# Row maxima of attention handed over in halves, and the expert weights of layer 0 loaded and turned at another place

## What is computed

```python
# layer 0 attention (layer 1: the same with a causal mask, without the three normalizations)
q, k, v = layernorm(x @ Wq + bq), layernorm(x @ Wk + bk), layernorm(x @ Wv + bv)   # per head
scores = einsum('bhqd,bhkd->bhqk', q, k) * HD ** -0.5
x = x + einsum('bhqk,bhkd->bqhd', softmax(scores), v).reshape(b, s, 256) @ Wo + bo
# layer 0 cross attention: top 32 of 77 scores, softmax over them, weighted values, output projection
# layer 0 experts
probs = softmax(einsum('bsd,ed->bse', x, router_w) + router_b)
y = take_along_axis(einsum('bsd,eod->bseo', x, expert_w) + expert_b, argmax(probs), axis=2)
x = x + y * max(probs)
```

## Time and profile before

| What | us |
|---|---|
| median of three runs (lowest, highest) | 1895.42 (1893.15, 1896.32) |
| the profiled execution | 1903.1 |
| its span | 1901.4 |
| attention of layer 0, first fill to last output half | 118.3 to 563.6 |
| from there to the first top-k instruction | 563.6 to 590.1 |
| attention of layer 1, first fill on | from 1132.1 |

### The profile page before, as it was taken

How to read it: one execution, slowest core, us unless ns; L and a number is a source line. 1 busy time by engine, 2 the same in 40 slices (tenths; PEclk the granted TensorE clock), 3 DMA queues, 4 the chain that set the end, 5 groups by cost and what they waited for, 6 DMA issues and landing times. The chain is left out here.

```text
span 1901.4 us, 27565 instructions
## 1 busy us (share of the span) xinstructions
PE 1543.4 (81%) x8891; PEld 836.8 (44%) x8892; DVE 1226.4 (64%) x4679; ACT 941.4 (50%) x1856; POOL 515.6 (27%) x419
## 2 busy tenths in 40 slices
PE   5858999999973688888877767999987883369997
PEld 3511222222222566666666533333326672136664
DVE  6978887877505999999992446777725567501211
ACT  2823777777663555555544432666673652111211
POOL 1791000000001466555553150111211332240111
PEclk9956999999897899999987876999998996679999
DMA  6293334221010000000000186355402122531110
GB/s 210 82 210 58 45 47 99 41 41 18 26 32 13 1 2 1 1 1 1 1 2 1 34 232 89 46 69 111 90 3 88 15 40 36 202 106 36 45 45 8
DMA packets 112679, 106.01 MB, mean 56 GB/s; under 512 B 45523, under 2 KB 86555, under 8 KB 112542
## 3 DMA queue, kind: packets, MB, share of 16 engines
q1 hardware_dynamic: 107281, 93.83, 23.4%
q0 software_dynamic: 2640, 6.31, 0.9%
q10 hardware_dynamic: 2624, 4.19, 0.7%
HBM read 68.56 MB, written 36.41 MB: 55 GB/s over the span
## 5 line engine op out<-in xcount | busy, mean ns | idle before, releaser
L1113 DVE TENSOR_REDUCE arena<-banks 128x2 f32<-128x1024 f32 (+1 forms) x448 | 481.2, 1107 | 162.2 <-PE banks L954 105.6
L1045 ACT ACTIVATE arena<-banks 128x512 f32<-128x512 f32 (+3 forms) x896 | 440.1, 557 | 188.1 <-PE banks L993 181.5
L954 PE MATMUL banks<-arena 96*128 96x512 bf16 (+3 forms) x896 | 286.4, 397 | 55.3 <-DMA arena<-v 26.8
L993 PE MATMUL banks<-arena 98*128 98x512 bf16 (+3 forms) x896 | 272.4, 364 | 9.3 <-ACT arena L1045 6.8
L1005 PE MATMUL banks<-arena 128*32 128x512 f32 (+3 forms) x1792 | 220.8, 565 | 12.6 <-ACT arena L1045 6.5
L1712 DVE MATCH_REPLACE8 arena<-arena 128x77 f32<-128x77 f32 x1024 | 213.8, 223 | 0.0
L954 PEld LDWEIGHTS banks<-arena 96*128 96x128 bf16 x896 | 80.8, 102 | 238.3 <-DVE arena L1113 137.7
L993 PEld LDWEIGHTS banks<-arena 98*128 98x128 bf16 x896 | 82.5, 98 | 188.5 <-ACT arena L1045 124.4
L1602 POOL TENSOR_SCALAR arena<-arena 128x256 f32<-128x256 f32 x32 | 39.2, 1224 | 449.8 <-DVE arena L1689 449.8
L2498 DVE COPY arena<-banks 128x1024 f32<-128x1024 f32 x23 | 28.2, 1225 | 198.6 <-PE banks L2432 198.6
L1704 DVE MAX8 arena<-arena 128x8 f32<-128x77 f32 x1024 | 149.5, 224 | 0.9
(11 more groups left out here) (279 smaller groups left out, 2465.3 us busy)
## 6 DMA issues: line engine op xcount, KB each, us to landing
arena<-parts SPq DMA_DIRECT2D x192, 128.0 KB, 7.4
parts<-arena SPq DMA_DIRECT2D x24, 512.0 KB, 5.3
arena<-in_L_ffn_W SPq DMA_DIRECT2D x12, 1024.0 KB, 10.9
v<-arena SPq DMA_DIRECT2D x32, 256.0 KB, 2.3
arena<-v SPq DMA_DIRECT2D x16, 512.0 KB, 11.1
arena<-in_L_ffn_W ACTq DMA_DIRECT2D x4, 1024.0 KB, 9.4
arena<-sorted_rows SPq DMA_DIRECT2D x23, 129.0 KB, 2.2
arena<-sorted SPq DMA_DIRECT2D x23, 128.0 KB, 2.1
```

Of the source, the lines that this page charges most:

```text
L954: mm = pe.matmul(bank[:, 0:w], qst[r][0:KS, j, i * P:(i + 1) * P], kst[r][0:KS, j, kb * BANK:kb * BANK + w], start=True, stop=not diag)
L993: pe.matmul(bank, kst[r][0:KM, j, kt * P:(kt + 1) * P], qst[r][0:KM, j, half * BANK + lo:(half + 1) * BANK], start=True, stop=True).then_i ...
L1045: act.activation(prob[:, gi % 2 * G + j, lo:BANK], PS[:, 4 + n % 3, 0:BANK - lo], ACT.Exp, scale=SCALE).then_inc(sem(s + "_exp"), 1)
L1113: dve.tensor_reduce(m2[u % 2][:, 2 * pair:2 * pair + 2, i, kb], PS[:, 2 * (n % 2):2 * (n % 2) + 2, 0:w], AX.X, ALU.max).then_inc(sem(s + " ...
```

## The change

Row maxima are handed over in two halves of four query tiles each. There are two MAX entries in a unit in place of one, each with its three small VectorE steps on half the elements, its own turn and copy, and four row DMAs (one for each head, 4 KB) in place of one. TensorE waits for the first half's rows before the unit's first group and for the second half's before the first group of the second query half. This holds for both layers. SyncE loads only unit 1 at the start, and unit 2 after both row halves of unit 0. In later units the load of unit u + 2 comes after the second half's rows of unit u.

In layer 0 alone the ring is dealt out anew: the second pass of unit 0 starts after fill 24 of unit 0 (`first_due`), and unit u ends at fill 28 of unit u + 1. In units 0 and 7 a quarter of the unit takes the entries up to MAX of the second half, and the rest is spread over the remainder.

The expert weights of layer 0 have memory of their own (`RAW_AT`), are loaded within attention at u = 4, and all eight are turned in iteration 0 (TURNS). Only the bias is loaded after attention.

```diff
@@ -856,7 +858,7 @@
             mx = [R.f32(G * TB).rearrange("p (j t) -> p j t", j=G) for _ in range(2)]
-            mh = [R.bf16(2 * G * TB) for _ in range(2)]
+            mh = [R.bf16(G * TB) for _ in range(2)]
             mT = [R.bf16(P) for _ in range(2)]
@@ -867,8 +869,11 @@
-            def hilo(u):
-                return mh[u % 2].rearrange("p (c j t) -> p c j t", c=2, j=G)
+            HT = TB // 2
+            HALF_FILLS = sum(1 for f in unit_fills if f[0] < HT)
+
+            def hilo(half):
+                return mh[half].rearrange("p (j c t) -> p c j t", c=2, j=G)
@@ -877,11 +882,24 @@
             for u in range(NU):
-                feed.insert(feed.index((FILL, u, NF - 1)) + (5 if u < NU - 1 else 1), (MAX, u, 0))
+                feed.insert(feed.index((FILL, u, HALF_FILLS - 1)) + 5, (MAX, u, 0))
+                feed.insert(feed.index((FILL, u, NF - 1)) + (5 if u < NU - 1 else 1), (MAX, u, 1))
+            first_due = feed.index((FILL, 1, AHEAD) if causal else (FILL, 0, 24))
             due = []
             for u in range(NU):
-                due.append(feed.index((FILL, u + 2, AHEAD)) if u + 2 < NU else len(feed))
-            first_due = feed.index((FILL, 1, AHEAD))
+                n, f = (u + 2, AHEAD) if causal else (u + 1, NF - 4)
+                due.append(feed.index((FILL, n, f)) if n < NU else len(feed))
+            early = 0.25
+
+            def goal(u, past):
+
+                at0 = due[u - 1] if u else first_due
+                if u in (0, NU - 1) and not causal:
+                    soon = max(at0, feed.index((MAX, u, 1)) + 1)
+                    if past <= early:
+                        return at0 + round((soon - at0) * past / early)
+                    return soon + round((due[u] - soon) * (past - early) / (1 - early))
+                return at0 + round((due[u] - at0) * past)
@@ -896,9 +914,9 @@
                         past += width(gi) / G
-                        goal = at0 + round((due[u] - at0) * past / WORK)
-                        ring += feed[at:goal]
-                        at = goal
+                        upon = goal(u, past / WORK)
+                        ring += feed[at:upon]
+                        at = upon
                         if j == 2 and gi in (1, last_of[0] + 2):
@@ -913,18 +931,26 @@
                 sp.wait_ge(sem(q + "_parts"), PARTS_ST)
-                for u in range(1, NST):
-                    load_unit(sp, l, u)
+                load_unit(sp, l, 1)
                 sp.wait_ge(sem(s + "_ones"), NST)
...
-                    sp.wait_ge(sem(s + "_red"), entry[MAX, u, 0] + 1)
-                    sp.dma_start(qst[u % NST][KS:KM], mT[u % 2][0:2 * G * TB]).then_inc(sem(s + "_rows"), 16)
-                    if 1 <= u <= NU - NST:
+                    for half in range(2):
+                        sp.wait_ge(sem(s + "_red"), entry[MAX, u, half] + 1)
+                        for j in range(G):
+                            sp.dma_start(qst[u % NST][KS:KM, j, half * BANK:(half + 1) * BANK], mT[half][j * 2 * HT:(j + 1) * 2 * HT]
+                                         ).then_inc(sem(f"{s}_rows{half}"), 16)
+                    if u == 0:
+                        load_unit(sp, l, 2)
+                    elif u <= NU - NST:
                         sp.wait_ge(sem(s + "_pv"), u * NGR)
...
                         clear(sp, rows_dram, NS * ROW, "rows_clear")
+                    if l == 0 and u == 4:
+                        for e in range(E):
+                            sp.dma_start(raw_experts[:, e], a["L0_ffn_expert_w"][e].rearrange("(k p) n -> p k n", p=P)
+                                         ).then_inc(sem("x0_we"), 16)
                     if l == 1 and u in (3, 5):
@@ -957,9 +983,9 @@
-                def turn_maxima(n, u):
-                    pe.wait_ge(sem(s + "_mh"), u + 1)
-                    pe.transpose(PS[0:2 * G * TB, 2 * (n % 2), 0:P // 2].bitcast(BF16), mh[u % 2], identb
+                def turn_maxima(n, u, half):
+                    pe.wait_ge(sem(s + "_mh"), 2 * u + half + 1)
+                    pe.transpose(PS[0:G * TB, 2 * (n % 2), 0:P // 2].bitcast(BF16), mh[half], identb
                                  ).then_inc(sem(s + "_fill"), 1)
@@ -978,7 +1004,7 @@
                         elif kind == MAX:
-                            turn_maxima(n, u)
+                            turn_maxima(n, u, f)
                         else:
@@ -1013,8 +1039,11 @@
                 for u in range(NU):
-                    pe.wait_ge(sem(s + "_rows"), 16 * (u + 1))
+                    pe.wait_ge(sem(s + "_rows0"), 16 * G * (u + 1))
                     for gi in range(NGR):
+                        if gi == last_of[0] + 1:
+                            first_pass(upto[u][gi * G])
+                            pe.wait_ge(sem(s + "_rows1"), 16 * G * (u + 1))
                         for j in range(G):
@@ -1083,18 +1112,22 @@
-                def maximum(u):
-                    dve.wait_ge(sem(s + "_red"), entry[FILL, u, NF - 1] + 1)
-                    dve.tensor_tensor(mx[u % 2], m2[u % 2][:, :, :, 0], m2[u % 2][:, :, :, 1], ALU.max).then_inc(sem(s + "_mx"), 1)
-
-                def high(u):
-                    dve.wait_ge(sem(s + "_mx"), u + 1)
-                    dve.tensor_scalar(hilo(u)[:, 0], mx[u % 2], -1.0, None, ALU.mult).then_inc(sem(s + "_mhi"), 1)
-
-                def low(u):
-                    dve.wait_ge(sem(s + "_mhi"), u + 1)
-                    dve.scalar_tensor_tensor(out=hilo(u)[:, 1], in0=mx[u % 2], scalar=-1.0, in1=hilo(u)[:, 0], op0=ALU.mult,
-                                             op1=ALU.subtract).then_inc(sem(s + "_mh"), 1)
+                def maximum(u, half):
+                    dve.wait_ge(sem(s + "_red"), entry[FILL, u, (HALF_FILLS, NF)[half] - 1] + 1)
+                    t = slice(half * HT, (half + 1) * HT)
+                    dve.tensor_tensor(mx[half][:, :, 0:HT], m2[u % 2][:, :, t, 0], m2[u % 2][:, :, t, 1], ALU.max
+                                      ).then_inc(sem(s + "_mx"), 1)
+
+                def high(u, half):
+                    dve.wait_ge(sem(s + "_mx"), 2 * u + half + 1)
+                    dve.tensor_scalar(hilo(half)[:, 0], mx[half][:, :, 0:HT], -1.0, None, ALU.mult).then_inc(sem(s + "_mhi"), 1)
+
+                def low(u, half):
+                    dve.wait_ge(sem(s + "_mhi"), 2 * u + half + 1)
+                    dve.scalar_tensor_tensor(out=hilo(half)[:, 1], in0=mx[half][:, :, 0:HT], scalar=-1.0, in1=hilo(half)[:, 0],
+                                             op0=ALU.mult, op1=ALU.subtract).then_inc(sem(s + "_mh"), 1)
+
+                steps = (maximum, high, low)
@@ -1112,20 +1145,17 @@
                                           AX.X, ALU.max).then_inc(sem(s + "_red"), 1)
-                        if f == 0 and u:
-                            maximum(u - 1)
-                        elif f == 1 and u:
-                            high(u - 1)
-                        elif f == 2 and u:
-                            low(u - 1)
+                        if f < len(steps) and u:
+                            steps[f](u - 1, 1)
+                        elif 0 <= f - HALF_FILLS < len(steps):
+                            steps[f - HALF_FILLS](u, 0)
                         elif (u, f) == (NU - 1, NF - 1):
-                            maximum(u)
-                            high(u)
-                            low(u)
+                            for step in steps:
+                                step(u, 1)
                     elif kind == MAX:
-                        if u >= 2:
-                            dve.wait_ge(sem(s + "_rows"), 16 * (u - 1))
-                        dve.tensor_copy(mT[u % 2][0:2 * G * TB], PS[0:2 * G * TB, 2 * (n % 2), 0:P // 2].bitcast(BF16)
+                        if u:
+                            dve.wait_ge(sem(f"{s}_rows{f}"), 16 * G * u)
+                        dve.tensor_copy(mT[f][0:G * TB], PS[0:G * TB, 2 * (n % 2), 0:P // 2].bitcast(BF16)
                                         ).then_inc(sem(s + "_red"), 1)
@@ -1211,10 +1243,10 @@
             bias = R.f32(D)[0:E]
-            spread = R.f32(2 * E * D)
+            spread = arena[:, RAW_AT:RAW_AT + 2 * E * D]
             hm = spread[:, 0:E * D].rearrange("p (e d) -> p e d", e=E)
             hmT = spread[:, E * D:].rearrange("p (c n) -> p c n", c=E * KD)
-            raw = spread.rearrange("p (e k n) -> p e k n", e=E, k=KD)
+            raw = raw_experts
             WeT = hT.rearrange("p k n -> p (k n)").rearrange("p (e k n) -> p e k n", e=E, k=KD)
@@ -1222,7 +1254,7 @@
             FIRST, LAST = -2, T + 3
-            TURNS = (3, 3, 2)
+            TURNS = (0, 0, E)
@@ -1245,10 +1277,8 @@
             def _(sp):
-                sp.wait_ge(sem("kblk"), 4 * B)
-                sp.wait_ge(sem(at + "_red"), NU * (len(fills(False)) + 3))
-                for e in range(E):
```

(3 more changed lines are left out.)

8 lines of the change are left out of this document (6 added, 2 removed).

## The result

The changed kernel takes 1880.3 us (median of 4 runs, 1879.9 to 1882.0) where the kernel before takes 1895.9 us beside it (4 runs, 1893.2 to 1898.0): ratio 0.9913, interval 0.9897 to 0.9929. It is faster by 16.5 us (13.5 to 19.5), at the slow end of the forecast's range (1861 to 1881) and not near its 25.6 us. The profiled execution took 1880.5 us, its span 1878.7.

The account below looks back on a forecast made before the run. VectorE was taken to bound the stretch ahead of unit 0, TensorE units 1 to 5. Terms of -15.0 (layer 0), -7.1 (cross stage) and -3.5 (layer 1) gave -25.6 us: 1895.4 to 1869.8 us, range 1861 to 1881.

Parts of the forecast that it names:

- Ahead of unit 0: Layer 0 before the second pass: 25 fills in place of 41, 16 x 1.18 = -18.9 us.
- Unit 0: Layer 0's first unit: 39 entries in place of 34, two of them at half clock, +4.3 us.
- Units 1 to 5: Layer 0's steady units: 50.1 us each with the added turn's group at 3.3, +4.0 us, bounds +1 and +8.
- Unit 6: Layer 0: 36 entries in place of 27, so 50.1 us like the units before it, +3.1 us.
- Unit 7: Layer 0's last unit: no wait for the row DMA and no half clock after it, 43.5 us, -7.5 us.
- Layer 0's attention: Sum of layer 0's attention terms: -15.0 us, bounds -19 and -10.
- Start of the cross stage: Attention's end to top-k: no weight wait or turns ahead, partly lost to half clock; -7.1 us, bounds -9.5 and -4.5.
- Layer 1: Layer 1's attention: row wait gone, one more turn per unit at 0.2 us; -3.5 us, bounds -5.5 and +1.
- The split rows: Four row DMAs per half: about 4 us, or 9.5 us if sequential, still under the 11.3 us of four groups.
- less comes through: Rival: new turns cost their upper bound in both layers, half clock takes most cross-stage gain; near 1880 us, chance 0.14.
- The stall in the middle of a unit: Rival: second half's rows land late, TensorE stops in layer 0's eight units, 44 us; 1914 us, chance 0.03.
- the late weights: Rival: expert weights or something else still hold the cross stage's start; -18.5 us, 1877 us, chance 0.06.

Follow-up runs that it names:

- e1: Kernel before with only layer 0's expert weights loaded at unit 4 and all turned in the first top-k step: ratio 0.9917, -15.8 us.
- e3: Changed kernel, but layer 1 turns whole maxima once per unit again, keeping the new order of loads: ratio 0.9852 to the kernel before, -28.2 us.
- e7: Changed kernel with expert weights loaded early but turned three, three and two beside the first tiles: ratio 0.9920 to the kernel before, -15.2 us.
- e2: Kernel before with only the load of unit 2 moved behind unit 0's rows, in both layers: ratio 0.9961, -7.4 us.
- e8: Changed kernel, layer 1's first-half maxima turned seven entries behind the half's last fill, not five: ratio 0.9906 to the kernel before, -17.9 us.
- e4: Changed kernel, layer 0's ring entries only beside the second and fourth matmul of a group: ratio 0.9850 to the kernel before, -28.6 us.
- c5: The changed kernel measured once more, unaltered: ratio 0.9909 to the kernel before, -17.3 us.
- e11: Changed kernel, layer 1's first-half turn seven entries behind the half's last fill, but five in the last unit: ratio 0.9881 to the kernel before, -22.6 us.

## Why the prediction was right in part

The sign and most mechanisms held; the size was 25.6 forecast, 18.6 in the stages of the profile, 16.5 in the runs. That 1880.3 us lies inside the range, 0.7 us from its end, is owed to the range's width and not to the sum, and the half clock in the gap brought the time towards that end: at full clock, as in e1 and e3, the gap is 5.5 us shorter.

- **Ahead of unit 0** (-18.9 forecast): -18.6. Sixteen reductions at VectorE's price.
- **Unit 0** (+4.3): 48.2 to 51.0, +2.7.
- **Units 1 to 5** (+4.0): 49.29 to 50.82, +7.7, next to the upper bound of 8. The mis-sized term is the group with a turn and two fills: taken as 3.3, it measured 3.68. The reason that I gave for the middle, that a turn in a fill's place shortened a group, was a wrong reading: there it replaced an entry, here it is the third, and the fill behind it waits for VectorE.
- **Unit 6** (+3.1): +3.9, the same group.
- **Unit 7** (-7.5): -4.8, 46.28 us. The mechanism held: no wait for rows, clock 1.00. The term "16 x 2.56" was miscounted: from 509.34 to 560.37 it is 17 groups, the last one of unit 6 and the 16 of unit 7. With 17 x 2.56 the same sum gives 46.0.
- **Layer 0's attention** (-15.0): -9.1, just outside the bound of -10.
- **Start of the cross stage** (-7.1): -7.9 in this profile, with the half clock that I had expected; the wait for the weights and the place of the turns both count, as e7 shows. At clock 1.00 it is -13.4 (e1), beyond my bound of -9.5. I had taken the times of before for all that stays, but that stretch ran at a mean clock of 0.77, so a full clock gives more than it had.
- **Layer 1** (-3.5): -1.6. The rows' wait went as forecast (e2: -7.1 for the order alone). The turn cost 0.57 us a unit and not 0.2, and more in the last two: +5.5 in all against e2's C. (The four profiles with this code in layer 1 have a C of 290.6 to 295.2, the four with whole maxima and the new order of loads 285.1 to 289.5; both spreads go with the clock.) The seventh interval at full clock has 30.09 us in after and 28.95 in e2, with a wait of 1.7 us at the turn in the one and 0.6 in the other. I had read its price off layer 0's rows, where no turn waits; in layer 1 its small steps stand between VectorE's reductions right ahead of it (e8).
- **The split rows**: no wait. The rule of the Trainium skill that I weighed (DMA: Bandwidth & Descriptors, section Bandwidth: batch, small transfers are dominated by descriptors) is about the time and bandwidth of the transfers themselves, and no row here gives those. What the traces show is a cost of issue, 2.6 us for a half in place of 0.52 for a unit, and four groups cover it. The pieces are 2.0 KB, and the single transfer of before has 16 KB, so both lie under the 64 KB that I quoted. A half sent as one transfer wasn't tried.

Of the rivals the first, less comes through, is what happened: its time was 1880, and its two causes, turns at their upper price and half clock in the cross stage, are the ones measured. I gave it 0.14. The stall in the middle of a unit and the late weights did not appear. Handing over in halves and dealing out layer 0's ring anew were only run together, so which of them gives the 9.1 us of layer 0 is not shown apart; the fewer fills ahead of unit 0 gave 18.6 us, unit 7 gave 4.8, and units 0 to 6 lost 14.3 of them again.

The profiled execution of before lay 7.7 us above its median. Between the two profiles the spans differ by 22.7 us, of which 18.6 lie in the three stages and 4.1 in the stretches between them, whose work is the same. The difference of two profiled executions is therefore not the gain; the sum over the stages touched comes closer here (18.6 against 16.5 in the runs).

## What to carry to other kernels

Where small work is woven into a chain of matmuls, count its price per place and not per piece: a third entry in a group cost 0.68 us as a fill and as a turn of maxima (1.06 in e4), though the turn's matmul alone takes 0.23, and moving the same entries to two of four places gave back 12.5 us, more than the change had gained there (9.1). The rule turned round in layer 1, where VectorE's reductions stood in the chain; try it for each stage. Take a change that has three parts apart: by stages the weights alone gave 13.4 us (e1, full clock), the order of loads 7.1 (e2), and the halves 9.1 in layer 0, of which they lost 5.5 again in layer 1. That would be 24.1 us; the gap's half clock took 5.5 of it, which leaves the 18.6 measured.

## What the runs showed of the hardware

The granted clock in a sparse stage is not fixed by the instructions up to it. The same instructions behind the same attention of layer 0 ran at a mean clock of 0.61, 0.61, 0.90, 0.82 and 1.00 (after, c5, e8, e11, e3), and the gap took 21.8, 21.9, 17.7, 19.0 and 16.3 us; the eight score matmuls take 2.32 us at the one level and 3.7 at the other. In after TensorE was at 1.2 GHz from the first projection at 554.41 (2.08 us for four matmuls) through the scores; in e8 that projection took 2.04 us too, but the next one, 5 us later, 1.13 us, at 2.4 GHz. The Trainium skill, TensorE: Matmul & The Clock Gate, Part 1, says that the number of matmuls at the low clock at a kernel's start differs from run to run of one kernel. The two kernels profiled twice repeat their gap, but in layer 1 after and c5, one kernel, differ as it says (1.00 and 0.94 in the seventh interval). In the gap the clock is worth up to 5.5 us, a third of this change's gain.
